# Attention maxima as two half-height matmuls side by side, four score banks, and the values one group later

## The chip, the cores and the metric

The kernel runs on one core of a Trainium2 chip. The metric is the device time of one launch in microseconds (us); lower is better. The core's engines are called PE (TensorE), DVE (VectorE), ACT (ScalarE), POOL (GpSimd) and SP (SyncE, which here only issues DMAs).

## The reference, cut to what matters

The program is two layers: a linear attention with a quantised feed-forward, then a softmax attention over 4096 tokens with 16 heads of 16, then a mixture of experts. The change touches only the softmax attention:

```
q, k, v = heads of layer_norm(x) @ Wq, Wk, Wv, with rotary positions on q and k     # 16 heads x 4096 x 16
p = softmax(q @ k.T * 16 ** -0.5)                                                   # 4096 x 4096 for each head
att = p @ v
```

## The kernel before

`attention` computes the softmax attention in bf16 products of split numbers. q and k are each the sum of three bf16 parts, and six products of parts (`Q_PART`, `K_PART`) stand under each other as rows of `QS` and `KS`: 6 x 16 = 96 rows (`ROWS`), so that one matmul over 96 rows sums all six. Two more rows hold the negative row maximum (in two bf16 parts) in `QS` and ones in `KS`, so that a score comes out of PE already shifted.

The work is 4 groups of 4 heads, and in each group 8 blocks of 512 queries: 32 blocks, numbered n. A block has 32 rounds (u), one for every 128 keys. In a round PE issues:
- four scores (`score`, L1068): 128 keys x 512 queries for one head each, into one of three PSUM banks `ST`. ACT takes the exponential of each (L1151) into the ring `PT` of 12.
- the values (`weigh`, L1083): four fp32 matmuls, one for each head, each on 32 of the array's columns, that sum into `OT`.
- two pairs of maxima matmuls (`max_pair`, L1049), for a *later* block: q times k over 96 rows, 128 queries x 512 keys twice, into a slot of two banks of `MP`. DVE takes one maximum over the 1024 numbers (L1179). There are two slots, so DVE can read one while PE fills the other.

The maxima of a block run 12 pairs (`LEAD`) and up to a block ahead. When all 64 pairs of the block are done, DVE makes the shift rows (`shifts`, L1184 to L1187), PE transposes them in round 29 (`negmax_transpose`), DVE copies them (`spread`), and SP puts them into `QS` (`store_negmax`). The output of the block before is copied out of `OT` by ACT (L1162), transposed by PE in round 2 (`out_transpose`, L1062), normalised by DVE (`normalise`, L1201 and L1203) and stored. Before the first block there is a head: SP loads group 0 and group 1 (`load_group`), and the 64 pairs of block 0 and 12 of block 1 run alone.

The order on each engine is the order of the code; semaphores carry the dependences. `mp_free` counts the maxima slots given back, `mp_full` those filled, `exp_done` the exponentials, `av_done` the rounds of values. ACT runs its 31 first blocks as a hardware loop (`act.Fori`, L1166), DVE its 30 first, PE six of the eight blocks of each group.

## Time and profile before

| | us |
|---|---|
| median of 3 runs (4894.16 to 4898.21) | 4896.37 |
| the profiled execution, its own time | 4870.05 |
| its span in the trace | 4868.0 |
| PE busy (93% of the span) | 4549.9 |
| DVE busy (63%) | 3049.8 |
| ACT busy (57%) | 2754.2 |
| POOL busy (8%) | 382.0 |

The profiled execution ran 26 us below the median, so durations read from it are summed against 4870.05. Busy PE time is an upper bound, since the ends of pipelined matmuls are modelled: what an instruction costs its successor is read from the starts. Shares are means over stages with different limits; the attention is the stretch from about 623 to 3782 us.

### The profile page before, as it was taken

The page shows a single profiled execution, that of the slowest core. Times are in us where ns is not written, and L with a number is a line of the kernel's source. Part 1 is how long each engine was busy: PE and PEld are TensorE (multiplying, and loading weights), DVE is VectorE, ACT ScalarE, POOL GpSimd, SP SyncE. Part 2 cuts the span into 40 slices and gives each one's busy share as a digit, 9 for nine tenths or more (in the row PEclk, how much of TensorE's full clock was granted, in tenths as well). Part 3 has the DMA queues.
Part 4 walks back from the last instruction along what each step waited for, and adds up shares of the span by engine and source line. Part 5 has one row for each costly group of instructions (what it writes and reads, how often), then busy time and mean ns, then how long its engine had stood idle before and what let it go on. Part 6 is the DMA issues. An engine that isn't in the chain of part 4 may idle for free. (4 is left out here: it accounts for less than half of the span.)

```text
span 4868.0 us, 75623 instructions
## 1 busy us (share of the span) xinstructions
PE 4549.9 (93%) x23944; PEld 2044.3 (42%) x23944; DVE 3049.8 (63%) x3267; ACT 2754.2 (57%) x5129; POOL 382.0 (8%) x364
## 2 busy tenths in 40 slices
PE   6888659999999999999999999999999799999999
PEld 4566402222222222222222222222222588886666
DVE  6777468888788878878887888888782011112222
ACT  4454306777777777777777777777778223222222
POOL 1233443000000000000000000000000100002110
PEclk8998759999999999999999999999999899999999
DMA  4222392000004000002200000000000655541111
GB/s 136 79 86 83 106 159 84 3 2 2 3 2 71 2 3 2 2 3 27 47 2 3 2 2 2 3 2 2 3 2 2 232 200 187 198 144 47 61 61 39
DMA packets 212703, 254.64 MB, mean 52 GB/s; under 512 B 35888, under 2 KB 183600, under 8 KB 210896
## 3 DMA queue, kind: packets, MB, share of 16 engines
q1 hardware_dynamic: 202544, 221.62, 16.3%
q0 software_dynamic: 9888, 30.04, 2.0%
q8 instruction: 93, 1.52, 0.1%
q14 instruction: 178, 1.46, 0.1%
HBM read 180.57 MB, written 70.78 MB: 52 GB/s over the span
## 5 line engine op out<-in xcount | busy, mean ns | idle before, releaser
L1179 DVE TENSOR_REDUCE a_MX<-a_MP 128x1 f32<-128x1024 f32 x2048 | 2415.8, 1220 | 584.3 <-PE a_MP L1049 577.3
L1151 ACT ACTIVATE a_PT<-a_ST 128x512 f32<-128x512 f32 x4096 | 2193.0, 598 | 970.6 <-PE a_ST L1068 904.6
L1068 PE MATMUL a_ST<-a_QS,a_KS 98*128 (+1 forms) x4096 | 1398.7, 385 | 70.3 <-ACT a_PT L1151 70.2
L1049 PE MATMUL a_MP<-a_KS,a_QS 96*128 96x512 bf16 x4096 | 1268.9, 392 | 58.1 <-DMA a_KS<-scr_kparts 44.5
L1083 PE MATMUL a_OT<-a_PT,a_VG 128*32 128x512 f32 x8192 | 1115.3, 617 | 0.1
L1068 PEld LDWEIGHTS a_ST<-a_QS,a_KS 98*128 98x128 bf16 x4096 | 394.9, 97 | 1272.0 <-ACT a_PT L1151 815.9
L1049 PEld LDWEIGHTS a_MP<-a_KS,a_QS 96*128 (+1 forms) x4096 | 385.9, 99 | 541.5 <-DVE a_MX L1179 130.7
L1384 ACT ACTIVATE e_hT<-e_up,e_BF 128x256 f32<-128x256 f32 x312 | 148.0, 474 | 409.8 <-PE e_up L1337 409.7
L1083 PEld LDWEIGHTS a_OT<-a_PT,a_VG 128*32 128x32 f32 x8192 | 162.0, 108 | 427.5 <-ACT a_PT L1151 388.3
L1337 PE MATMUL e_up<-e_xT,e_WF 128*128 128x256 f32 x1248 | 323.5, 382 | 0.8 <-DVE e_xT L1394 0.8
L1346 PE MATMUL e_dn<-e_WP,e_hT 128*128 128x256 f32 x1248 | 321.3, 380 | 0.0
L1346 PEld LDWEIGHTS e_dn<-e_WP,e_hT 128*128 128x128 f32 x1248 | 237.7, 191 | 33.1
L1337 PEld LDWEIGHTS e_up<-e_xT,e_WF 128*128 128x128 f32 x1248 | 236.2, 192 | 32.2 <-DVE e_xT L1394 1.2
L1280 POOL MEMSET e_ident<- 128x128 f32 x1 | 0.2, 204 | 2981.6 <-POOLq L908 2981.6
L1394 DVE COPY e_xT<-e_tp 128x512 f32<-128x512 f32 x39 | 27.0, 692 | 297.1 <-PE e_tp L1330 297.1
L1672 DVE TENSOR_TENSOR u_Y<-u_w,t_XN 128x512 f32<-128x512 f32 x16 | 11.1, 692 | 313.6 <-PE u_w L1577 313.6
L1401 DVE TENSOR_TENSOR e_Y<-e_dn,e_BP 128x256 f32<-128x256 f32 x78 | 32.1, 424 | 235.5 <-PE e_dn L1346 235.3
L342 ACT ACTIVATE f_E<-f_F 128x512 f32<-128x512 f32 x128 | 79.4, 620 | 137.9 <-PE f_F L581 137.9
L1646 ACT ACTIVATE u_hT<-u_a,t_bfs 128x512 f32<-128x512 f32 x64 | 44.0, 687 | 187.1 <-PE u_a L1589 187.1
L1646 ACT ACTIVATE u_hT<-u_a,t_b1c 128x512 f32<-128x512 f32 x64 | 44.0, 687 | 164.7 <-PE u_a L1589 164.7
L467 DVE SCALAR_TENSOR_TENSOR f_QP<-f_E,f_R 128x512 f32<-128x512 f32 x128 | 99.4, 801 | 46.9 <-ACT f_R L343 46.6
L1599 PE MATMUL u_d<-t_wps,u_hT 128*128 128x256 f32 x512 | 121.0, 379 | 0.0
(219 smaller groups left out, 2796.2 us busy)
## 6 DMA issues: line engine op xcount, KB each, us to landing
e_WF<-Wfc SPq DMA_DIRECT2D x39, 1024.0 KB, 5.0
e_WP<-Wproj SPq DMA_DIRECT2D x39, 1024.0 KB, 7.1
a_QS<-scr_qparts SPq DMA_DIRECT2D x192, 64.0 KB, 14.9
a_KS<-scr_kparts SPq DMA_DIRECT2D x24, 512.0 KB, 19.3
scr_xs<-f_zero SPq DMA_DIRECT2D x1, 9984.0 KB, 32.8
e_XS<-scr_xs SPq DMA_DIRECT2D x39, 256.0 KB, 2.7
scr_ys<-e_Y SPq DMA_DIRECT2D x39, 256.0 KB, 2.1
f_X<-x SPq DMA_DIRECT2D x16, 512.0 KB, 4.8
```

The costliest lines, as they stand in the source:

```text
L342: A.activation(E[:, u % ER, :], F[:, j, :], ACT.Exp)
L467: V.scalar_tensor_tensor(QP[:, g // 2 * 4 + j, g % 2, :], E[:, u % ER, :], 1.0, R[:, u % ER, :], ALU.min, ALU.add).then_inc(S["feat"], 1)
L1049: last = T.matmul(MP[:, slot, i, :], QS[j][0:ROWS, bass.ds((b * HG + h) * BLK + t * P, P)], KS[j][0:ROWS, h, (kb + i) * BLK:(kb + i + 1) * ...
L1068: T.matmul(ST[:, bank_of(c), :], KS[j][:, h, u * P:(u + 1) * P], QS[j][:, bass.ds((b * HG + h) * BLK, BLK)], start=True, stop=True).then_i ...
L1083: last = T.matmul(OT[w, :], VG[j][:, u, w], PT[:, (HG * u + h) % RING, :], start=u == 0, stop=u == KT - 1)
L1151: nc.scalar.activation(PT[:, c % RING, :], ST[:, bank_of(c), :], ACT.Exp, scale=SOFT_SCALE).then_inc(S["exp_done"], 1)
L1179: V.reduce_max(MX[:, x:x + 1], MP[:, slot, :, :].rearrange("p a n -> p (a n)"), AX.X).then_inc(S["mp_free"], 1)
L1337: last = T.matmul(UP[:, m % UPB, 0:ET], WF[j][:, k, m * P:(m + 1) * P], xT[j][:, k, :], start=k == 0, stop=k == DC - 1)
L1346: last = T.matmul(DN[:, t, 0:D], hT[j][:, m, t * P:(t + 1) * P], WP[j][:, m, :], start=m == 0, stop=m == HC - 1)
L1384: nc.scalar.activation(hT[j][:, m, :], UP[:, m % UPB, 0:ET], ACT.Gelu_apprx_tanh, bias=BF[j][:, m:m + 1]).then_inc(S["hid_ready"], 1)
L1599: last = T.matmul(DN[:, t // 2, t % 2 * D:(t % 2 + 1) * D], hT[:, u % HR, t * P:(t + 1) * P], down_w[half][:, m, :], start=u == 0 and t % ...
L1646: nc.scalar.activation(hT[:, u % HR, :], A[:, use % BANKS, :], ACT.Relu if u >= HC else ACT.Gelu_apprx_tanh, bias=(tt["b1c"] if u >= HC el ...
```

## The change

The rows of `QS` and `KS` are laid out anew, on all 128 rows. For the first two heads of a group (side 0) the first four products stand in rows 0 to 63, the last two in rows 64 to 95 and the shift rows from row 96; for the other two heads (side 1) the four products stand in rows 64 to 127, the two in rows 0 to 31 and the shifts from row 32. The rows left over are zero in `QS` (POOL writes them once).

A pair of maxima is now one head of each side for the same 512 keys: two matmuls over 64 rows each, one on the upper and one on the lower half of the array's rows, each into a bank of its own. The maximum is taken over four products, not six (it only shifts the exponent, so the softmax stays the same). `MP` is three single banks in a ring instead of two double ones; DVE takes one maximum over 512 numbers for each bank, and `mp_free` counts banks. The bank that this frees makes a fourth score bank.

A round on PE is now pair, values, pair, four scores; the values are those of the group of four scores before, and the last values of a block are issued in the first round of the next one. PE and DVE are written out without loops; ACT keeps its loop. Loads of `QS` and `KS` and the store of the shifts are split by side, so there are twice as many DMAs of half the size, and the head's first maxima wait for the four leading products only.

```
-STACK = ROWS + SHIFTS
+HALF = 64
+LEADING = HALF // HD1
+SIDES = HG // 2
 CHUNKS = HG * KT
-SBANKS = 3
-PAIRS = HG * TPB * KB // 2
+SBANKS, MBANKS = 4, 3
+PAIRS = HG // 2 * TPB * KB
 LEAD = 12
 TURN_OUT = 2
 TURN_MAX = 29
-EVENTS = PAIRS + 2
-HEAD_EVENTS = PAIRS + 1 + LEAD
+EVENTS = SIDES * PAIRS + 2
...
+HEAD_EVENTS = SIDES * (PAIRS + LEAD) + 1
...
-EXPS = 2 * SBANKS
...
-    return max(c for c in range(chunk - 2 * SBANKS, chunk) if bank_of(c % CHUNKS) == bank_of(chunk))
+def main_row(side, r):
+    return HD1 * r + HALF * side if r < LEADING else HD1 * (r - LEADING) + HALF * (1 - side)
+def shift_row(side):
+    return HALF * (1 - side) + HD1 * (len(Q_PART) - LEADING)
+def first_event(n):
+    return HEAD_EVENTS + n * EVENTS - (SIDES * LEAD if n == NG * NB - 1 else 0)
...
-        MP = pb("MP", [P, 2, 2, BLK])
+        MP = pb("MP", [P, MBANKS, BLK])
         OT = pb("OT", [P, BLK])
-        def negT_ps(slot):
-            return MP[:, slot, 0, :].bitcast(bf16)[0:SHIFTS * HG * TPB, 0:P]
+        def bank(e):
+            return MP[:, e % MBANKS, :]
...
-                nc.gpsimd.memset(KS[j][ROWS:STACK, :, :], 1.0).then_inc(S["ones_ok"], 1)
-                pool.wait_ge(S["ones_ok"], j + 1)
...
+                for side in range(SIDES):
+                    r0, h0 = shift_row(side), side * HS
+                    nc.gpsimd.memset(KS[j][r0:r0 + WIN, h0:h0 + HS, :], 1.0).then_inc(S["ones_ok"], 1)
+                    nc.gpsimd.memset(QS[j][r0:r0 + WIN, :].rearrange("r (b h n) -> r b h n", b=NB, h=HG)[:, :, h0:h0 + HS, :],
+                                     0.0).then_inc(S["ones_ok"], 1)
+            pool.wait_ge(S["ones_ok"], 4 * SIDES)
...
+                for side in range(SIDES):
+                    h0, row = G * HG + side * HS, main_row(side, r)
+                    heads, c0 = slice(h0 * HD1, (h0 + HS) * HD1), (b * HG + side * HS) * BLK
+                    sp.dma_start(QS[G % 2][row:row + HD1, c0:c0 + HS * BLK].rearrange(
+                        "e (h n) -> e h n", h=HS), scr["qparts"][Q_PART[r], heads, b * BLK:(b + 1) * BLK].rearrange(
+                        "(h e) n -> e h n", e=HD1)).then_inc(sem, 16)
...
-                early = S["first"] if G == 0 else load[G % 2]
                 for r in range(len(Q_PART)):
+                    early = S["first"] if G == 0 and r < LEADING else load[G % 2]
                     load_q(G, r, 0, early)
...
-                sp.dma_start(QS[j][ROWS:STACK, bass.ds(b * HG * BLK, HG * BLK)], negT[:]).then_inc(S["negmax_load"], 16)
+                for side in range(SIDES):
+                    rows = SHIFTS * HS * TPB
+                    sp.dma_start(QS[j][shift_row(side):shift_row(side) + SHIFTS, bass.ds((b * HG + side * HS) * BLK, HS * BLK)],
+                                 negT[side * rows:(side + 1) * rows, :]).then_inc(S["negmax_load"], 16)
...
+            sp.wait_ge(S["ones_ok"], 4 * SIDES)
             store_negmax(0, 0, 0)
...
-                room(e)
-                for i in range(2):
-                    last = T.matmul(MP[:, slot, i, :], QS[j][0:ROWS, bass.ds((b * HG + h) * BLK + t * P, P)],
-                                    KS[j][0:ROWS, h, (kb + i) * BLK:(kb + i + 1) * BLK], start=True, stop=True)
-                last.then_inc(S["mp_full"], 1)
...
+                h, t, kb = x // (TPB * KB), x // KB % TPB, x % KB
+                room(e + SIDES - 1)
+                for side in range(SIDES):
+                    hs, half = side * HS + h, slice(side * HALF, (side + 1) * HALF)
+                    T.matmul(bank(e + side), QS[j][half, bass.ds((b * HG + hs) * BLK + t * P, P)],
+                             KS[j][half, hs, kb * BLK:(kb + 1) * BLK], start=True, stop=True).then_inc(S["mp_full"], 1)
...
-            def score(n, j, b, c):
-                u, h = c // HG, c % HG
-                pe.wait_ge(S["exp_done"], n * CHUNKS + freed_by(c) + 1 + EXPS)
-                T.matmul(ST[:, bank_of(c), :], KS[j][:, h, u * P:(u + 1) * P],
-                         QS[j][:, bass.ds((b * HG + h) * BLK, BLK)], start=True, stop=True).then_inc(S["qk_done"], 1)
-            def score_first(n, j, b):
-                pe.wait_ge(S["negmax_load"], 16 * (n + 1))
-                for c in range(SBANKS):
-                    score(n, j, b, c)
-            def weigh(n, j, u):
-                pe.wait_ge(S["exp_done"], n * CHUNKS + HG * u + HG - 1 + EXPS + 1)
...
+            def scores(n, j, b, u):
+                for c in range(HG * u, HG * (u + 1)):
+                    pe.wait_ge(S["exp_done"], n * CHUNKS + c + 1)
+                    h = c % HG
+                    T.matmul(ST[:, c % SBANKS, :], KS[j][:, h, u * P:(u + 1) * P],
+                             QS[j][:, bass.ds((b * HG + h) * BLK, BLK)], start=True, stop=True).then_inc(S["qk_done"], 1)
+            def scores_first(n, j, b):
+                pe.wait_ge(S["negmax_load"], 16 * SIDES * (n + 1))
+                scores(n, j, b, 0)
+            def weigh(n, u):
+                j = n // NB % 2
+                pe.wait_ge(S["exp_done"], n * CHUNKS + HG * (u + 1) + SBANKS)
...
                 for u in range(KT):
-                    for x in range(2 * u, 2 * u + 2):
+                    for x in (2 * u, 2 * u + 1):
                         if x < PAIRS - LEAD and next1:
-                            max_pair(first + k, (HEAD_EVENTS + k) % 2, *next1, x + LEAD)
-                            k += 1
+                            max_pair(e, *next1, x + LEAD)
+                            e += SIDES
                         if x >= PAIRS - LEAD and next2:
-                            max_pair(first + k, (HEAD_EVENTS + k) % 2, *next2, x - PAIRS + LEAD)
-                            k += 1
+                            max_pair(e, *next2, x - PAIRS + LEAD)
+                            e += SIDES
                         if x % 2 == 0:
-                            score(n, j, b, HG * u + SBANKS)
                             if u:
-                                weigh(n, j, u - 1)
+                                weigh(n, u - 1)
+                            elif n:
+                                weigh(n - 1, KT - 1)
                             if u == TURN_OUT:
-                                out_transpose(first + k, (HEAD_EVENTS + k) % 2, n)
-                                k += 1
+                                out_transpose(e, n)
+                                e += 1
                             if u == TURN_MAX and next1:
-                                negmax_transpose(first + k, (HEAD_EVENTS + k) % 2, n + 1)
-                                k += 1
-                            if u < KT - 1:
-                                score(n, j, b, HG * u + SBANKS + 1)
+                                negmax_transpose(e, n + 1)
+                                e += 1
                     if u < KT - 1:
-                        score(n, j, b, HG * u + SBANKS + 2)
-                        score(n, j, b, HG * u + SBANKS + 3)
-                if next1:
-                    score_first(n + 1, *next1)
-                weigh(n, j, KT - 1)
-            pe.wait_ge(S["ident_ok"], 1)
-            pe.wait_ge(S["ones_ok"], 2)
+                        scores(n, j, b, u + 1)
+                    elif next1:
+                        scores_first(n + 1, *next1)
...
-                with pe.Fori(0, NB - 2) as b:
+                for b in range(NB - 2):
...
+            weigh(NG * NB - 1, KT - 1)
+            out_transpose(first_event(NG * NB - 1) + 1, NG * NB)
...
+            def maximum(e, x):
+                for side in range(SIDES):
+                    dve.wait_ge(S["mp_full"], e + side + 1)
+                    V.reduce_max(MX[:, side, x:x + 1], bank(e + side), AX.X).then_inc(S["mp_free"], 1)
...
-            with dve.Fori(0, NG * NB - 2) as n:
-                one_block(n, True, True)
...
+            blocks = NG * NB
+            for n in range(blocks):
+                one_block(n, n + 1 < blocks, n + 2 < blocks)
```

On PE, one round in the middle of a block. Before (`a_ST` are the scores, `a_MP` the maxima, `a_OT` the values):

```order
L1068 MATMUL a_ST<-a_QS,a_KS 128x512
L1049 MATMUL a_MP<-a_KS,a_QS 128x512 x2
L1068 MATMUL a_ST<-a_QS,a_KS 128x512 x2
L1049 MATMUL a_MP<-a_KS,a_QS 128x512 x2
L1068 MATMUL a_ST<-a_QS,a_KS 128x512
L1083 MATMUL a_OT<-a_PT,a_VG 32x512 x4
```

And one round on PE now:

```order
L1073 MATMUL a_MP<-a_KS,a_QS 128x512 x2
L1106 MATMUL a_OT<-a_PT,a_VG 32x512 x4
L1073 MATMUL a_MP<-a_KS,a_QS 128x512 x2
L1092 MATMUL a_ST<-a_QS,a_KS 128x512 x4
```

The scores moved together at the round's end, and the values stand between the two pairs.

On PE, where a block ends and the next begins, with the semaphores that each waits for. Before:

```order
L1068 MATMUL a_ST<-a_QS,a_KS 128x512 [waits a_exp_done,a_negmax_load]
L1068 MATMUL a_ST<-a_QS,a_KS 128x512 [waits a_exp_done] x2
L1083 MATMUL a_OT<-a_PT,a_VG 32x512 [waits a_exp_done]
L1083 MATMUL a_OT<-a_PT,a_VG 32x512 x3
L1049 MATMUL a_MP<-a_KS,a_QS 128x512 [waits a_mp_free]
L1049 MATMUL a_MP<-a_KS,a_QS 128x512
L1068 MATMUL a_ST<-a_QS,a_KS 128x512 [waits a_exp_done] x2
L1049 MATMUL a_MP<-a_KS,a_QS 128x512 [waits a_mp_free]
L1049 MATMUL a_MP<-a_KS,a_QS 128x512
```

And the same place on PE now:

```order
L1092 MATMUL a_ST<-a_QS,a_KS 128x512 [waits a_exp_done,a_negmax_load]
L1092 MATMUL a_ST<-a_QS,a_KS 128x512 [waits a_exp_done] x3
L1073 MATMUL a_MP<-a_KS,a_QS 128x512 [waits a_mp_free]
L1073 MATMUL a_MP<-a_KS,a_QS 128x512
L1106 MATMUL a_OT<-a_PT,a_VG 32x512 [waits a_exp_done]
L1106 MATMUL a_OT<-a_PT,a_VG 32x512 x3
L1073 MATMUL a_MP<-a_KS,a_QS 128x512 [waits a_mp_free]
L1073 MATMUL a_MP<-a_KS,a_QS 128x512
L1092 MATMUL a_ST<-a_QS,a_KS 128x512 [waits a_exp_done] x4
```

Between the block's last values and the first scores that need an exponential from beyond ACT's jump there was one pair and three scores; the last values now come behind the first pair of the next block.

## Rows read from the trace of the kernel before

**Rows 1.** The page's groups: line, engine, operation, count, busy us, mean ns, idle before

```profile
L1179 DVE TENSOR_REDUCE a_MX<-a_MP 128x1 f32<-128x1024 f32 x2048 | 2415.8, 1220 | 584.3 <-PE a_MP L1049 577.3
...
L1394 DVE COPY e_xT<-e_tp 128x512 f32<-128x512 f32 x39 | 27.0, 692 | 297.1 <-PE e_tp L1330 297.1
...
L1401 DVE TENSOR_TENSOR e_Y<-e_dn,e_BP 128x256 f32<-128x256 f32 x78 | 32.1, 424 | 235.5 <-PE e_dn L1346 235.3
```

**Rows 2.** Timeline of one round: start us, us, engine, what, count, idle before

```profile
3650.30 0.39 PE L1068 MATMUL a_ST<-a_QS,a_KS 98*128 98x512 bf16 x1
...
3650.53 0.60 PE L1049 MATMUL a_MP<-a_KS,a_QS 96*128 96x512 bf16 x2
...
3650.81 2.15 ACT L1151 ACTIVATE a_PT<-a_ST 128x512 f32<-128x512 f32 x4 [0.69 <-PE a_ST L1068]
...
3651.16 2.36 DVE L1179 TENSOR_REDUCE a_MX<-a_MP 128x1 f32<-128x1024 f32 x2 [0.48 <-PE a_MP L1049]
...
3651.83 0.38 PE L1068 MATMUL a_ST<-a_QS,a_KS 98*128 98x512 bf16 x1
...
3652.14 1.06 PE L1083 MATMUL a_OT<-a_PT,a_VG 128*32 128x512 f32 x8
...
3653.14 0.39 PE L1068 MATMUL a_ST<-a_QS,a_KS 98*128 98x512 bf16 x1
```

**Rows 3.** Timeline where one block ends and the next begins, and one block later

```profile
1222.91 0.60 ACT L1162 COPY a_OS<-a_OT 128x512 f32<-128x512 f32 x1
...
1225.64 1.57 ACT L1151 ACTIVATE a_PT<-a_ST 128x512 f32<-128x512 f32 x3 [2.13 <-issue]
...
1226.39 0.39 PE L1068 MATMUL a_ST<-a_QS,a_KS 98*128 x1 [2.00 <-ACT a_PT L1151]
...
1318.41 0.60 ACT L1162 COPY a_OS<-a_OT 128x512 f32<-128x512 f32 x1
```

**Rows 4.** Busy time by stretch; PEclk is the granted clock as a share

```profile
core 0: us, PE busy (x) PEld busy (x) DVE busy (x) ACT busy (x) POOL busy (x), PEclk, DMA share, GB/s
1224.30:1226.40 2.10, 0.10 (x2) 0.01 (x1) 1.40 (x2) 0.76 (x2) 0.00 (x0) 1.00 0.01 4
1226.40:1229.70 3.30, 3.30 (x12) 0.63 (x12) 1.22 (x1) 1.91 (x4) 0.00 (x0) 0.56 0.00 0
3710.00:3770.00 60.00, 53.56 (x303) 11.60 (x301) 0.68 (x2) 51.63 (x100) 0.00 (x0) 1.00 0.01 3
623.00:640.00 17.00, 0.00 (x0) 0.00 (x0) 0.00 (x0) 0.00 (x0) 16.94 (x2) 0.50 0.98 115
```

**Rows 5.** Groups with shapes, 1000 to 1500 us: DVE's work once in a block

```profile
L1203 DVE TENSOR_TENSOR a_AO<-a_MP,a_rd 128x256 f32<-128x256 f32 x5 | 2.1, 425 | 0.7
L1184 DVE TENSOR_REDUCE a_neg<-a_MX 128x16 f32<-128x64 f32 x6 | 1.3, 220 | 0.2
L1201 DVE RECIPROCAL a_rd<-a_MP 128x16 f32<-128x16 f32 x5 | 1.3, 258 | 1.6 <-PE a_MP L1062 1.6
```

**Rows 6.** Timeline of PE in round 2 of block 0: the output's transposes

```profile
757.13 0.66 PE L1062 MATMUL a_MP<-a_identf,a_OS 128*128 128x128 f32 x4
757.62 0.38 PE L1068 MATMUL a_ST<-a_QS,a_KS 98*128 x1
```

**Rows 7.** Timeline of the head: first load issued, first maxima, last load issued

```profile
623.09 0.35 SPq L981 DMA_DIRECT2D a_QS<-scr_qparts  x1
...
656.81 1.86 PE L1049 MATMUL a_MP<-a_KS,a_QS 96*128 96x512 bf16 x4 [44.53 <-DMA a_KS<-scr_kparts]
...
657.86 75.31 DVE L1179 TENSOR_REDUCE a_MX<-a_MP 128x1 f32<-128x1024 f32 x64 [35.41 <-PE a_MP L1049]
...
725.89 0.46 SPq L992 DMA_DIRECT2D a_VG<-scr_va  x1
```

**Rows 8.** Timeline of ACT: the last block's start, one of its rounds, its end

```profile
3704.01 0.60 ACT L1162 COPY a_OS<-a_OT 128x512 f32<-128x512 f32 x1
...
3712.68 2.06 ACT L1151 ACTIVATE a_PT<-a_ST 128x512 f32<-128x512 f32 x4 [0.33 <-PE a_ST L1068]
...
3780.64 0.59 ACT L1162 COPY a_OS<-a_OT 128x512 f32<-128x512 f32 x1 [1.19 <-PE a_OT L1083]
```

More of the change, by code:

```diff
@@ L1189, in spread @@
-            def spread(n, e, slot, after):
-                dve.wait_ge(S["mp_full"], e + 1)
-                if after:
-                    dve.wait_ge(S["negmax_load"], n * 16)
-                V.tensor_copy(negT[:], negT_ps(slot)).then_inc(S["negmaxT_copied"], 1)
+            dve.sem_inc(S["mp_free"], MBANKS)
+            def maximum(e, x):
+                for side in range(SIDES):
+                    dve.wait_ge(S["mp_full"], e + side + 1)
+                    V.reduce_max(MX[:, side, x:x + 1], bank(e + side), AX.X).then_inc(S["mp_free"], 1)
@@ L1194, in spread, with normalise @@
+            def spread(n, e):
+                dve.wait_ge(S["mp_full"], e + 1)
+                if n:
+                    dve.wait_ge(S["negmax_load"], n * 16 * SIDES)
+                V.tensor_copy(negT[:], negT_ps(e)).then_inc(S["negmaxT_copied"], 1)
                 dve.wait_ge(S["negmaxT_copied"], n + 1)
                 dve.sem_inc(S["mp_free"], 1)
-            def normalise(n, e, slot):
+            def normalise(n, e):
                 dve.wait_ge(S["mp_full"], e + 1)
-                o4 = MP[:, slot, 0, :].rearrange("p (t h e) -> p t h e", t=TPB, h=HG)
+                o4 = bank(e).rearrange("p (t h e) -> p t h e", t=TPB, h=HG)
@@ L1208, in one_block @@
             def one_block(n, more1, more2):
-                c.base, c.n, k = FIRST + n * STEPS, 0, 0
-                first = HEAD_EVENTS + n * EVENTS - (0 if more1 else LEAD)
+                e = first_event(n)
                 for u in range(KT):
-                    for x in range(2 * u, 2 * u + 2):
+                    for x in (2 * u, 2 * u + 1):
                         if x < PAIRS - LEAD and more1:
-                            maximum(first + k, (HEAD_EVENTS + k) % 2, x + LEAD)
-                            k += 1
+                            maximum(e, x + LEAD)
+                            e += SIDES
@@ L1216, in one_block @@
                             if x == PAIRS - LEAD - 1:
-                                shifts(n + 1, first + k - 1)
+                                shifts(e)
                         if x >= PAIRS - LEAD and more2:
-                            maximum(first + k, (HEAD_EVENTS + k) % 2, x - PAIRS + LEAD)
-                            k += 1
+                            maximum(e, x - PAIRS + LEAD)
+                            e += SIDES
                         if x == 2 * TURN_OUT:
-                            normalise(n, first + k, (HEAD_EVENTS + k) % 2)
@@ L1223, in one_block @@
-                            k += 1
+                            normalise(n, e)
+                            e += 1
                         if x == 2 * TURN_MAX and more1:
-                            spread(n + 1, first + k, (HEAD_EVENTS + k) % 2, True)
-                            k += 1
+                            spread(n + 1, e)
+                            e += 1
             for x in range(PAIRS):
-                maximum(x, x % 2, x)
-            shifts(0, PAIRS - 1)
-            spread(0, PAIRS, PAIRS % 2, False)
+                maximum(SIDES * x, x)
@@ L1232, in _ @@
+            shifts(SIDES * PAIRS)
+            spread(0, SIDES * PAIRS)
             for x in range(LEAD):
[L1233 to L1241 removed]
```

99 lines of the change are left out of this document (43 added, 56 removed).

## The prediction

> **What bounds the kernel now.** I read the page's groups first. DVE's maxima are its costliest work, 2048 of 1220 ns, yet DVE was idle 577 us of its time waiting for PE's maxima [rows 1]. So DVE is not the bound; it is second in line. The timeline of one round says the same with starts: PE goes from score to score in 3653.14 - 3650.30 = 2.84 us without a hole, DVE works 2.36 of that and waits 0.48, ACT 2.15 and waits 0.69 [rows 2]. PE is the bound of a round. Its parts: two matmuls of 512 columns end 0.60 after the first starts and one alone takes 0.385, so one costs its successor 0.215; eight of them (four scores, four maxima) are 1.72. From the last score to the values it is 0.31 (3652.14 - 3651.83), 0.10 above 0.215. The values take 1.00 to the next start. 1.72 + 0.10 + 1.00 = 2.82.
>
> Then the timeline at a block's end. From copy to copy a block takes 1318.41 - 1222.91 = 95.50 us [rows 3], against 32 rounds of 2.84 = 90.9. Of the 4.6 left, 0.49 are the output's transposes (757.62 - 757.13) [rows 6]. Most of the rest starts at ACT: after its copy it jumps back in its loop and takes its next exponential 2.73 us later (1225.64 - 1222.91), and PE stands 2.00 us for it [rows 3]. Right behind that hole PE's granted clock is 0.56 for 3.3 us, where it had been 1.00: half of the time it is at 1.2 instead of 2.4 GHz [rows 4]. That costs about 3.3 x 0.44 = 1.5 us of PE's work.
>
> **What the change does to PE's round.** A pair of maxima stands on two halves of the rows. If the halves run at once, a pair costs one matmul, 0.215, and not two. No row shows two row halves. The nearest are the values, which use four column strips of 32: four fp32 matmuls in 1.00 us [rows 2], and the trace counts eight passes of 512 columns in them; one after another at 0.215 they would be 1.72, so strips do run at once. I take 0.245 (0.03 for loading the second half's weights, an estimate). Bounds: 0.215, and 0.43 if the halves don't overlap.
>
> Against that, PE changes its tiling more often. Before, it did so twice in a round: into the values (+0.10) and out of them (1.00 less 4 x 0.215 is 0.14, an estimate, if the values stream as long as four scores). Now it is four times: maxima to values, values to maxima, maxima to scores, scores to maxima. I price the two new ones at 0.12 each, the mean of the two known. The sum: 0.245 + 0.10 + 1.00 + 0.245 + 0.12 + 0.86 + 0.12 = 2.69, say 2.70. With changes at 0.10 and a pair at 0.215 it is 2.59; with new changes at 0.20 and a pair at 0.245 it is 2.85.
>
> The Trainium skill, "TensorEngine Tiling (Array Packing)", Key Properties, says that changing the tiling mode drains TensorE, which speaks against this order of the round; the extra 0.10 and 0.14 beside the values agree. By its Theoretical Speedup a contraction of up to 64 gives up to 2x, so it expects the halves to overlap.
>
> **DVE's round.** It now takes four maxima over 512 numbers for two over 1024. A read of 512 instead of 256 numbers costs 692 - 424 = 268 ns more, so 512 numbers are 536 ns [rows 1]. One maximum alone is then 1220 - 536 = 684 ns. In the head 64 of the long ones ran back to back in 75.31 us, 1.177 each [rows 7]; short ones back to back are 0.641, four are 2.56. DVE's floor is below PE's 2.70, but only by 0.14, where it was 0.48.
>
> Does the ring of three banks let both run? Let pair A start at 0. DVE can start 0.42 after the last matmul of a pair (3651.16 - 3650.53 - 0.215) [rows 2], so at about 0.45. PE reaches pair B at 0.245 + 0.10 + 1.00 = 1.35; B needs A's first bank, which is read at 0.45 + 0.68 = 1.13. B is there at 1.80, DVE is through with A at 1.73. The next A comes at 2.70 and needs B's first bank, read at 2.48. So both handovers fit with about 0.2 us to spare, and PE sets the round. But only 0.2: before, a whole slot was between them.
>
> So DVE's work once in a block is no longer covered. Normalising is 258 + 425 ns and two waits on itself, some 0.85 [rows 5], beside 0.49 of transposes on PE [rows 6]; DVE reads the next pair only after that, I count 1.0 for both. The shifts are 220 ns and three small ones behind it, 0.85, of which 0.2 is covered: 0.65. Spread and its transpose: 0.3. Together 2.0 a block.
>
> **The block's end.** ACT still loops, so the 2.73 us from copy to next exponential stay. But the last values now stand behind the first pair of the next block, and four scores are out already. With that pair at 0, the values start at 0.35, the copy at about 1.6, ACT's next exponential at 4.3, done at 4.9. PE meanwhile has a pair, four scores whose banks are free, a pair, the values of group 0 and a pair; it comes to the first score that needs that exponential at 4.4, and then takes one score for each exponential, 0.52 apart (2.15 less 0.60, by three), instead of 0.215. The stall is 0.5 + 3 x 0.3 = 1.4 us instead of 2.0, and in pieces. I add 0.6 for a clock that falls behind some of them: 2.0.
>
> A block is 32 x 2.70 + 2.0 + 2.0 = 90.4, which is 5.1 less than 95.5. There are 31 such, 158 us.
>
> **Last block.** No maxima there: 3780.64 - 3704.01 = 76.6 us, of which each round is 2.06 of exponentials and 0.33 of waiting for a score [rows 8]. With four banks and the values a group behind, PE's 1.96 (0.10 + 1.00 + 0.86) lies beside ACT's 2.07, so about 32 x 2.07 + 1 = 67: 9 us. The six rounds without maxima before it give 1 more.
>
> **Head.** Loads are bound by the DMA engines, 0.98 busy from 623 to 640 us [rows 4], so half-size DMAs of the same bytes cost the same. The first maxima wait for four of six products: two thirds of the 33.7 us from 623.09 to 656.81, 11 us sooner [rows 7]. At the head's 1.2 GHz [rows 4] the ring of three is too short: DVE needs 1.28 for a pair, and a pair of matmuls at this clock is ready 657.86 - 656.81 - 0.43 = 0.62 after its last one starts. With 0.03 for the halves and 0.05 for the semaphore (estimates) that is 0.70 from the end of a first read, a little over the 0.64 of the second read that covers it. So about 1.33 against 1.177, times 76 pairs: 12 us more. Net nothing. SP issues 218 DMAs instead of 109 ahead of the first shifts. It took 103 us for the 109 (725.89 - 623.09), held up by full DMA engines; one issue by itself is 0.35 long [rows 7], so 218 are at least 76 us and may still fit. I take nothing, with up to +20. POOL's extra clearing lies beside the head.
>
> **Sum.** -158 - 9 - 1 + 0 = -168 against 4870.05, so 4702. The median stood 26 us above the profiled execution: 4728, say 4725.
>
> **Rivals.**
> - *The halves don't overlap.* A pair costs 0.43, the round 2.69 + 2 x 0.185 = 3.06, a block 102; 31 x 6.5 - 10 = +190: about 5085. For it: no row shows row halves. Against: the column strips do overlap. It decides from a pair above 0.33. Chance 0.06.
> - *The handover is the bound.* If the new changes of tiling cost 0.20, or a bank comes back 0.2 us later than I count, each pair waits: 2.85 a round, a block 95.2, about 4875. For it: only 0.2 to spare, DVE 95% full. Against: PE's waits in the head are short. Chance 0.12, half of it within 0.2% of no change or slower.
> - *The block's end stays as it is.* The clock falls at every end and PE waits as before, 2 us a block more: 4725 + 60 = 4785. Chance 0.14.
> - *SP's queue.* If issuing costs by the DMA and not by the byte, the first shifts wait for up to 100 us more behind group 1's loads: about 4790. Chance 0.04.
> - *The clock falls in the rounds.* PE is then full 2.13 of 2.70; but in the last block it ran at clock 1.00 with 1.72 of 2.39 [rows 4, 8]. Half clock would be slower, over 5500. Chance 0.01.
> - *As forecast*: 0.63.
>
> **How the numbers follow.** A measurement of this kernel tells about 0.2% from no change, 10 us. Faster: 0.63 + 0.14 + 0.04 + half of 0.12 = 0.87. Slower: 0.06 + 0.01 + 0.02 = 0.09. Same: 0.04. The forecast's own range comes from the round: 2.59 gives 4725 - 31 x 32 x 0.11 = 4616, and 2.76 gives 4785. The handover rival ends at 4875. Cutting the low end at 4640 and the high end at 4840 leaves about 2 in 10 out.
>
> **What would show it.** In the changed trace: the two matmuls of a pair start within 0.05 us of each other and the pair costs its successor under 0.3; a round is 2.70 from values to values; DVE's short maximum is 684 ns and DVE is over 90% busy in the attention; ACT's copy-to-exponential gap still 2.7 us but PE's idle behind it under 1 us in one piece; a block 90.4, the last one 67. I am wrong if a change of tiling costs much more than 0.12, or if PE is seen waiting for DVE before most pairs.

## The result, and the profile after

The changed kernel takes 4626.88 us (median of 4 runs, 4626.26 to 4627.09) against 4895.26 us (4 runs, 4885.17 to 4898.21) for the kernel before on the same chip: a ratio of 0.9451, 95% interval 0.9437 to 0.9466. The prediction was 4725 with a range from 4640 to 4840. The sign was right, the time is 98 us under the forecast and 13 us under the range. The profiled execution took 4626.26 us, so the gain between profiled executions is 243.8 us where 168 were worked out.

The page's groups of the changed kernel, in the columns of [rows 1]:

```profile
L1199 DVE TENSOR_REDUCE a_MX<-a_MP 128x1 f32<-128x512 f32 x4096 | 2631.5, 685 | 144.9 <-PE a_MP L1073 84.2
L1171 ACT ACTIVATE a_PT<-a_ST 128x512 f32<-128x512 f32 x4096 | 2108.4, 605 | 810.4 <-PE a_ST L1092 519.3
```

DVE's idle time in front of its maxima fell from 584 us [rows 1] to 145: the spare time is gone, and a short maximum is 685 ns where 684 was worked out.

The timeline of one round of the changed kernel, as [rows 2] for before:

```profile
1501.28 0.39 PE L1073 MATMUL a_MP<-a_KS,a_QS 64*128 64x512 bf16 x2
...
1501.60 1.07 PE L1106 MATMUL a_OT<-a_PT,a_VG 128*32 128x512 f32 x8
...
1502.60 0.39 PE L1073 MATMUL a_MP<-a_KS,a_QS 64*128 64x512 bf16 x2
...
1502.92 1.04 PE L1092 MATMUL a_ST<-a_QS,a_KS 128*128 128x512 bf16 x4
1503.43 1.57 ACT L1171 ACTIVATE a_PT<-a_ST 128x512 f32<-128x512 f32 x3 [0.55 <-PE a_ST L1092]
1503.89 0.39 PE L1073 MATMUL a_MP<-a_KS,a_QS 64*128 64x512 bf16 x2
```

The x2 of a pair spans 0.39, as one matmul alone did in [rows 2], where two in a row spanned 0.60: the halves run at once, with no lag to be seen. From the starts a round is 0.32 + 1.00 + 0.32 + 0.97 = 2.61 us, and nothing in it waits. The four scores are 4 x 0.215 = 0.86 of the 0.97, the pair 0.215 of each 0.32. So each change of tiling next to a pair costs 0.10 to 0.11.

The end of a block in the changed kernel, to be held against [rows 3]; the last row is the copy one block later:

```profile
1212.99 0.59 ACT L1182 COPY a_OS<-a_OT 128x512 f32<-128x512 f32 x1
...
1215.39 0.39 PE L1073 MATMUL a_MP<-a_KS,a_QS 64*128 64x512 bf16 x2
1215.65 4.03 ACT L1171 ACTIVATE a_PT<-a_ST 128x512 f32<-128x512 f32 x8 [2.08 <-PE a_OT L1106]
...
1216.30 1.86 PE L1092 MATMUL a_ST<-a_QS,a_KS 128*128 128x512 bf16 x4 [0.53 <-ACT a_PT L1171]
...
1218.09 0.39 PE L1073 MATMUL a_MP<-a_KS,a_QS 64*128 64x512 bf16 x2
...
1300.09 0.59 ACT L1182 COPY a_OS<-a_OT 128x512 f32<-128x512 f32 x1
```

From ACT's copy to its next exponential it is 2.66 us, nearly as before (2.73). PE stands 0.53 in one piece and then takes a score for each exponential: from pair to pair it is 2.70 (1218.09 - 1215.39) where a group of scores otherwise takes 1.29 (1503.89 - 1502.60), so 1.41 are lost. A block is 1300.09 - 1212.99 = 87.10 us, 8.4 less than [rows 3].

Busy time by stretch, in the columns of [rows 4]: 500 us of full blocks, then the stretches at and behind PE's wait.

```profile
1000.00:1500.00 500.00, 480.13 (x2913) 124.14 (x2968) 480.16 (x776) 381.19 (x741) 0.00 (x0) 1.00 0.05 7
...
1215.60:1218.90 3.30, 2.47 (x16) 0.64 (x14) 1.85 (x4) 3.25 (x7) 0.00 (x0) 1.00 0.01 2
1218.90:1222.00 3.10, 2.69 (x19) 0.92 (x12) 2.62 (x6) 1.93 (x5) 0.00 (x0) 1.00 0.01 2
```

DVE is 0.96 busy, and the granted clock stays 1.00 behind the block's end, where it was 0.56 before [rows 4]. The busy share overstates how full DVE is: a maximum is 0.69 long in the trace, but where DVE has maxima to catch up on (behind the normalising, at 1220.96) they start 0.60 to 0.61 apart. Four of them take about 2.43 of the round's 2.61, so DVE has some 0.18 to spare in each round.

The copies of the last blocks and ACT inside the last one, as [rows 8]:

```profile
3390.52 0.59 ACT L1182 COPY a_OS<-a_OT 128x512 f32<-128x512 f32 x1
3472.58 0.62 ACT L1182 COPY a_OS<-a_OT 128x512 f32<-128x512 f32 x1
...
3499.57 12.88 ACT L1171 ACTIVATE a_PT<-a_ST 128x512 f32<-128x512 f32 x26
...
3535.74 0.58 ACT L1182 COPY a_OS<-a_OT 128x512 f32<-128x512 f32 x1 [1.19 <-PE a_OT L1106]
```

The last block is 63.16 us against 76.6. ACT no longer waits in it: exponentials in a row cost 12.88 / 26 = 0.495 each, 1.98 a round. The block ahead of it is 82.06.

The head of the changed kernel, as [rows 7]:

```profile
621.79 0.81 SPq L998 DMA_DIRECT2D a_QS<-scr_qparts  x2
...
642.34 0.61 PE L1073 MATMUL a_MP<-a_KS,a_QS 64*128 64x512 bf16 x2 [31.34 <-DMA a_KS<-scr_kparts]
643.73 0.61 PE L1073 MATMUL a_MP<-a_KS,a_QS 64*128 64x512 bf16 x2 [0.78 <-DVE a_MX L1199]
...
733.30 0.21 DVE L1214 COPY a_negT<-a_MP 32x128 bf16<-32x128 bf16 x1 [0.56 <-issue]
737.78 0.43 SPq L1011 DMA_DIRECT2D a_VG<-scr_va  x1
738.33 6.26 SPq L1030 DMA_DIRECT2D a_QS<-a_negT  x2
...
750.69 1.49 PE L1092 MATMUL a_ST<-a_QS,a_KS 128*128 128x512 bf16 x3 [1.60 <-DMA a_QS<-a_negT]
```

First maxima 20.6 us behind the first load, against 33.7 in [rows 7]; pairs at 1.39; the shifts ready at 733.5 and on their way only at 738.33, behind SP's last load. PE stands 1.60 us for them.

Between first scores and first copy, block 0 showed something that the trace of before did not have:

```profile
785.41 0.96 POOL L983 DMA_INDIRECT scr_xs<-a_XR,g_slot  x1 [0.30 <-issue]
786.26 1.29 DVE L1199 TENSOR_REDUCE a_MX<-a_MP 128x1 f32<-128x512 f32 x2 [2.42 <-remote]
786.40 2.06 ACT L1171 ACTIVATE a_PT<-a_ST 128x512 f32<-128x512 f32 x4 [2.67 <-remote]
...
787.01 0.39 PE L1073 MATMUL a_MP<-a_KS,a_QS 64*128 64x512 bf16 x2 [2.20 <-issue]
```

DVE, ACT and PE stand still together, released by nothing that the trace names ("remote", "issue"), again and again while POOL scatters token rows for the experts (it does so from 688 to 817 us). All three are idle at once in six places of more than 0.5 us before the first copy, 0.7 to 2.8 us each; the rest of the loss is waits of one engine at a time. The first copy stands at 864.57 in place of 842.77.

### The profile page after: what moved, and what is told of

It reads as the page before. It is cut to its first block and busy times, and to the rows that moved or that the text cites. A ratio compares the mean times of both kernels' runs of the same rounds, so it can differ in the third digit from the quotient of the medians.

```text
span 4624.5 us, 70156 instructions
## 1 busy us (share of the span) xinstructions
PE 4221.0 (91%) x23643; PEld 1849.4 (40%) x23944; DVE 3267.1 (71%) x5315; ACT 2670.8 (58%) x5129; POOL 409.1 (9%) x370
## 5 line engine op out<-in xcount | busy, mean ns | idle before, releaser
L1199 DVE TENSOR_REDUCE a_MX<-a_MP 128x1 f32<-128x512 f32 x4096 | 2631.5, 685 | 144.9 <-PE a_MP L1073 84.2
L1171 ACT ACTIVATE a_PT<-a_ST 128x512 f32<-128x512 f32 x4096 | 2108.4, 605 | 810.4 <-PE a_ST L1092 519.3
L1106 PE MATMUL a_OT<-a_PT,a_VG 128*32 128x512 f32 x8192 | 1093.9, 606 | 1.2 <-ACT a_PT L1171 0.9
L1092 PE MATMUL a_ST<-a_QS,a_KS 128*128 128x512 bf16 x3795 | 1033.4, 383 | 56.9 <-ACT a_PT L1171 23.6
L1073 PE MATMUL a_MP<-a_KS,a_QS 64*128 64x512 bf16 x4096 | 817.0, 396 | 153.8 <-DVE a_MX L1199 105.7
L1073 PEld LDWEIGHTS a_MP<-a_KS,a_QS 64*128 64x128 bf16 x4096 | 196.9, 93 | 1403.3 <-DVE a_MX L1199 1341.0
L1092 PEld LDWEIGHTS a_ST<-a_QS,a_KS 128*128 128x128 bf16 x4096 | 319.9, 98 | 551.4 <-ACT a_PT L1171 279.3
```

What stands on the lines that cost most here:

```text
L1073: T.matmul(bank(e + side), QS[j][half, bass.ds((b * HG + hs) * BLK + t * P, P)], KS[j][half, hs, kb * BLK:(kb + 1) * BLK], start=True, sto ...
L1092: T.matmul(ST[:, c % SBANKS, :], KS[j][:, h, u * P:(u + 1) * P], QS[j][:, bass.ds((b * HG + h) * BLK, BLK)], start=True, stop=True).then_i ...
L1106: last = T.matmul(OT[w, :], VG[j][:, u, w], PT[:, (HG * u + h) % RING, :], start=u == 0, stop=u == KT - 1)
L1171: nc.scalar.activation(PT[:, c % RING, :], ST[:, c % SBANKS, :], ACT.Exp, scale=SOFT_SCALE).then_inc(S["exp_done"], 1)
L1199: V.reduce_max(MX[:, side, x:x + 1], bank(e + side), AX.X).then_inc(S["mp_free"], 1)
```

## The experiments

Ratios are against the kernel before on the same chip. The runs were made on three chips. On one the kernel before takes 4867 us: there ran the experiments with both matmuls on one half, with half maxima, with ACT written out (first run) and with the late scatter. On the two others it takes 4891. The changed kernel itself was not run on the first chip, so what is held against it there goes by the ratio and by the length of a block, not by the time. The base for all is the changed kernel, run again on one of the two others:

> The changed kernel itself once more (one blank line added), as the base for the runs beside it. If the changed kernel's time is a fixed share of the kernel before's on any chip: ratio 0.945. In block 0 the first profile had holes of 1 to 3.5 us in which DVE, ACT and PE stood still together, some 22 us in all. Theory 1, the holes belong to that one execution or chip: none here, the first copy of OT 842 to 850 us into the span. Theory 2, they belong to the kernel (the scatter runs beside block 0): the first copy near 864 us and a hole of over 1 us wherever the scatter runs.

Measured: 4626.22 us, ratio 0.9459 [0.9446, 0.9472]; first copy at 859.88, blocks 87.10, last block 63.15. The holes showed again.

### Do the two halves run at once?

```
-                for side in range(SIDES):
+                side = x % 2
+                for i in range(2):
+                    y = x // 2 * 2 + i
+                    h, t, kb = y // (TPB * KB), y // KB % TPB, y % KB
                     hs, half = side * HS + h, slice(side * HALF, (side + 1) * HALF)
-                    T.matmul(bank(e + side), QS[j][half, bass.ds((b * HG + hs) * BLK + t * P, P)],
+                    T.matmul(bank(e + i), QS[j][half, bass.ds((b * HG + hs) * BLK + t * P, P)],
```

> The two maxima matmuls of a pair stand on the same half of the rows (two key blocks of one head) and not on both halves; the work and the order are otherwise the changed kernel's. If the gain of a round comes from the two halves running at once, the second matmul costs 0.215 again: a round 2.61 + 2 x 0.215 = 3.04 us, the kernel 4627 + 992 x 0.43 = about 5055 us. Rival, the gain comes from the order and the banks alone: 4627, no change.

Measured: 4976.59 us, ratio 1.0233 [1.0216, 1.0250]. PE's timeline:

```profile
1500.65 0.60 PE L1075 MATMUL a_MP<-a_KS,a_QS 64*128 64x512 bf16 x2
1501.18 1.06 PE L1108 MATMUL a_OT<-a_PT,a_VG 128*32 128x512 f32 x8
1502.18 0.60 PE L1075 MATMUL a_MP<-a_KS,a_QS 64*128 64x512 bf16 x2
1502.71 1.04 PE L1094 MATMUL a_ST<-a_QS,a_KS 128*128 128x512 bf16 x4
1503.68 0.60 PE L1075 MATMUL a_MP<-a_KS,a_QS 64*128 64x512 bf16 x2
```

On one half the pair spans 0.60 and costs 0.215 more (0.53 to the values in place of 0.32), the round is 3.03, as expected. A block is 99.43, 12.3 more and not 13.8: beyond its 32 rounds a block now has 2.4 us where it had 3.6, which fits that a slower PE covers part of DVE's work once in a block again. So the halves do overlap, wholly, and without that the change would have made the kernel slower. The rival that they don't is refuted.

### Does PE or DVE set the round?

```
-                    V.reduce_max(MX[:, side, x:x + 1], bank(e + side), AX.X)
+                    V.reduce_max(MX[:, side, x:x + 1], bank(e + side)[:, 0:BLK // 2], AX.X)
```

> DVE takes its maxima over 256 of the 512 numbers (so the shift is not the row's true maximum); the output changes only by rounding. If PE sets the round, it stays 2.61 us and only DVE's once-a-block work gets covered: a block 87.1 to about 85.5, the head's 76 pairs shorter by 0.27 each, in all some 4555. Rival, DVE (96% busy) sets the round: it falls by more than 0.05, and the kernel below 4520.

Measured: 4563.79 us, ratio 0.9382 [0.9363, 0.9401]; DVE 0.58 busy from 1000 to 1500 us, the starts in a round unchanged (0.32, 1.00, 0.32, 0.97), a block 85.70. It leaves out half of each maximum. PE sets the round; of the block, 1.4 us are DVE's. The ratio is 0.008 above what the expectation comes to (4555 of 4895), and half of that is the head: the shifts were ready at 719.1, but SP's store of them stood behind its loads. SP's and PE's timeline, up to 752 us:

```profile
739.59 6.11 SPq L1030 DMA_DIRECT2D a_QS<-a_negT  x2
...
751.43 1.06 PE L1092 MATMUL a_ST<-a_QS,a_KS 128*128 128x512 bf16 x2 [19.66 <-DMA a_QS<-a_negT]
```

From first load to first scores it was 127.8 us, where the changed kernel takes 128.9: faster maxima do not shorten the head, since SP's queue is right behind them.

### What does a change of tiling cost?

```
                         if x % 2 == 0:
+                            if u < KT - 1:
+                                scores(n, j, b, u + 1, 0, 2)
                             if u:
                                 weigh(n, u - 1)
...
-                        scores(n, j, b, u + 1)
+                        scores(n, j, b, u + 1, 2, HG)
```

> The first two of the four scores stand ahead of the values, so that a round has five changes of tiling (pair to scores, scores to values, values to pair, pair to scores, scores to pair) and not four, with the same matmuls. Theory: each change costs PE 0.10 us: the round 2.61 to 2.71, a block 87.1 to 90.3, in all some 100 us slower than the control. By the 0.12 of the prediction it would be 120 us slower. Rival: a change costs nothing by itself, and what stands ahead of the values (0.32 from pair to values) is theirs: round 2.61, no difference.

Measured: 5058.55 us, ratio 1.0341 [1.0325, 1.0356]: four times the loss that was expected. PE's timeline shows where:

```profile
1500.56 0.39 PE L1073 MATMUL a_MP<-a_KS,a_QS 64*128 64x512 bf16 x2
1500.88 0.61 PE L1092 MATMUL a_ST<-a_QS,a_KS 128*128 128x512 bf16 x2
1501.74 0.39 PE L1073 MATMUL a_MP<-a_KS,a_QS 64*128 64x512 bf16 x2 [0.24 <-DVE a_MX L1201]
1502.06 0.60 PE L1092 MATMUL a_ST<-a_QS,a_KS 128*128 128x512 bf16 x2
1502.59 1.07 PE L1106 MATMUL a_OT<-a_PT,a_VG 128*32 128x512 f32 x8
1503.59 0.39 PE L1073 MATMUL a_MP<-a_KS,a_QS 64*128 64x512 bf16 x2
```

The steps without a wait are 0.32 or 0.53 (2 x 0.215 + 0.10) or 1.00: a fifth change is 0.10 again. But the two pairs now stand 1.18 and 1.85 apart, and the first distance is a wait for a bank. The round is 3.03, 0.10 from the change and 0.32 from the handover. A block is 100.5, 13.4 more, and 1.1 to 1.6 longer still where the granted clock falls at its end, which it does behind 22 of the 30 ends: of the 432 us that were lost, some 30 are the clock. What the 0.10 of a change is made of, no run takes apart. To part the change from the wait, the same order with a shorter read:

```
 five changes as above, and
+                    V.reduce_max(MX[:, side, x:x + 1], bank(e + side)[:, 0:BLK // 2], AX.X)
```

> The round with five changes of tiling again (two of the four scores ahead of the values), now with DVE's maxima over 256 of the 512 numbers (it leaves half of each maximum out), so that a bank comes back sooner. In the run with whole maxima the starts read 0.32 from pair to scores, 0.53 for two scores, 1.00 for the values: 0.10 for each change, in sum 2.71 a round, and 0.32 more of waiting for a bank, since a pair can follow a pair only 1.18 behind it (0.43 until DVE starts, 0.68 its read, 0.07 back to PE). Theory: with the read at 0.42 that falls to 0.92, nothing waits, and the round is 2.71 against 2.61 of the half maxima alone: a block 85.7 + 3.2 = 88.9, ratio 0.938 + 0.021 = 0.959. Rival: the wait is not for a bank but part of the changes themselves: round 3.03 as with whole maxima, ratio about 1.03.

Measured: 4789.86 us, ratio 0.9798 [0.9783, 0.9813]. The round went from 3.03 to 2.76: the wait was for the bank, since only DVE's read was shortened. Of the 0.05 over 2.71, all stands between the two pairs that are close (0.90 apart, under the 0.92 that I had worked out), so a trace of the wait is left. The total missed 0.959: a block is 92.2, not 88.9. Its rounds are 88.3; 2.2 is what the block with half maxima alone has beyond its rounds (85.7 - 83.5, of which 1.4 is the block's end); and 1.7 is new. Most of it stands at the block's end: with two scores ahead of the values PE comes sooner to a score that needs an exponential from beyond ACT's jump, and stands 2.2 to 2.5 us in one piece (2.42 at 1053.39) where it stood 0.5. Besides, 7 of the 29 full blocks are 1.3 to 1.6 longer still; in just these the granted clock falls at the end (below).

### What the fourth score bank is worth

```
-SBANKS, MBANKS = 4, 3
+SBANKS, MBANKS, EARLY = 3, 3, 4
...
-                    pe.wait_ge(S["exp_done"], n * CHUNKS + c + 1)
+                    pe.wait_ge(S["exp_done"], n * CHUNKS + freed_by(c) + 1 + EXPS)
...
-                    T.matmul(ST[:, c % SBANKS, :], KS[j][:, h, u * P:(u + 1) * P],
+                    T.matmul(ST[:, bank_of(c), :], KS[j][:, h, u * P:(u + 1) * P],
```

(`bank_of` is the chunk modulo 3, `freed_by` the chunk that read the bank last.)

> Three score banks in place of four (the maxima keep their three single banks, one bank of PSUM lies idle), all else as changed. Theory: the fourth bank is what lets the four scores stand together. With three, the fourth score of a group waits for the exponential of the first, which is ready about 0.51 + 0.61 us behind its score (score to exponential, one exponential), where the fourth score would start 0.65 behind it: some 0.45 us more in every round, 2.61 to about 3.05, and a block 87.1 to about 101; in all 31 x 14 = 430 us slower than the control. Rival: the scores stand in a queue with slack and PE makes up for the wait in the values: round 2.61, under 40 us slower.

Measured: 5153.52 us, ratio 1.0533 [1.0515, 1.0552], 527 us over the control. The fourth score waits for the first exponential:

```profile
1539.66 0.82 PE L1102 MATMUL a_ST<-a_QS,a_KS 128*128 128x512 bf16 x3
1540.82 0.39 PE L1102 MATMUL a_ST<-a_QS,a_KS 128*128 128x512 bf16 x1 [0.34 <-ACT a_PT L1181]
1541.14 0.39 PE L1083 MATMUL a_MP<-a_KS,a_QS 64*128 64x512 bf16 x2
```

It starts 1.16 behind the first in place of 0.65: 0.51 more, a round of 3.12. The direction and the mechanism were as expected, the size 0.07 a round short. (At 12 of the 30 block ends the clock falls too, for 1.3 us each.) The last block is 76.12 there, as before the change (76.6 [rows 8]), against 63.15 in the control: that saving belongs to the fourth bank.

### The block's end and the clock

```
-            with act.Fori(0, NG * NB - 1) as n:
+            for n in range(NG * NB - 1):
```

> ACT's blocks are written out, without its loop. If the stall at a block's end is ACT's jump, 1.4 us of each of 30 ends go: 4627 - 42 = 4585, and a block 85.7. Rival, ACT would start no sooner because it waits for the values or the copy: 4627.

Measured: 4556.96 us, ratio 0.9362 [0.9347, 0.9378]; on another chip (second run, below) 0.9375 [0.9362, 0.9387]. A block is 85.68, 1.42 less: the whole of PE's loss at the block's end is ACT's jump. (In us it is less than the 4585 that were expected since it ran on the chip where the kernel before takes 4867.)

Whether such a wait also costs clock, I tried by making it longer: ACT takes two exponentials of the next block ahead of its jump, not four.

```
-                for c in range(SBANKS, CHUNKS):
+                for c in range(2, CHUNKS):
...
-                    for c in range(SBANKS):
+                    for c in range(2):
```

> ACT takes only two of the next block's exponentials ahead of its copy and jump, not four. The same work, but PE then has less to do while ACT jumps, so it stands in one long hole at each block's end instead of pieces: about 1.2 us more standing. Theory, from the kernel before (2.00 us of standing still, then the clock at 0.56 for 3.3 us): one hole of 2 to 3 us brings the granted clock down behind it, and a block is 87.1 + 1.2 + 1.5 = 89.8, in all some 80 us slower than the control. Rival, the clock stays 1.00 whatever PE does here: 87.1 + 1.2 = 88.3, some 37 us slower.

Measured: 4695.36 us, ratio 0.9601 [0.9586, 0.9616], 69 us over the control, between the two expectations, and the blocks say why. Two block ends, PE's hole in each, and the clock behind it:

```profile
1045.55 0.88 PE L1092 MATMUL a_ST<-a_QS,a_KS 128*128 128x512 bf16 x2 [2.80 <-ACT a_PT L1171]
...
1226.22 0.88 PE L1092 MATMUL a_ST<-a_QS,a_KS 128*128 128x512 bf16 x2 [2.72 <-ACT a_PT L1171]
```

```profile
1047.00:1050.00 3.00, 3.00 (x14) 0.54 (x6) 2.35 (x4) 1.76 (x4) 0.00 (x0) 0.56 0.00 0
...
1227.00:1229.00 2.00, 2.00 (x15) 0.56 (x15) 1.52 (x3) 1.61 (x4) 0.00 (x0) 1.00 0.00 0
```

Nearly the same hole, and once the clock falls to 1.2 GHz for most of the next 3 us, once it stays at 2.4. Of the 29 full blocks 16 are 88.7 to 89.0 and 13 are 90.1 to 90.5: 1.5 us for a fallen clock, behind 13 of 29 holes. 29 x 1.7 + 13 x 1.5 = 69. So a hole of this length does not always cost clock, and pieces of 0.5 to 0.8, as in the changed kernel, never did: its clock is 1.00 behind every block end, and its full blocks are 87.1 to 87.3 in both runs.

Nor does the length decide it. Counted over the 30 block ends of each trace, the clock fell behind 29 in the kernel before (holes of 1.8 to 2.2 us), behind 22 with five changes (1.9 to 2.2), behind 7 with five changes and half maxima (2.2 to 2.5), behind 12 with three banks (2.4 to 2.7) and behind 13 here (2.6 to 2.9). What decides whether one of these holes costs clock was not found.

### The holes of block 0

```
             pool.wait_ge(S["ones_ok"], 4 * SIDES)
+            pool.wait_ge(S["av_done"], 4 * KT)
             for b in range(NB):
```

> POOL's scatter of rows to the experts waits until three blocks are done; before, it ran beside the head and block 0, where PE, DVE and ACT stand still together for 1 to 3.5 us at a time, 27 us in all. If the scatter's DMAs hold up the instruction fetch of the written-out code, the holes move with it, and the time stays at 4627 +- 5. If the holes belong to the start of the attention and need more than the scatter, they are gone from block 0 and don't come back: about 4602.

Measured: 4604.53 us, ratio 0.9466 [0.9450, 0.9482]: no gain. The chip was one without holes: its neighbours, with the scatter beside block 0, had none either (first copies 841 to 850), and the moved scatter made none (blocks 87.1 to 87.5). It was tried again, with ACT written out, beside ACT written out alone:

> ACT written out, and POOL's scatter of token rows starts behind block 3 instead of beside the head and block 0. Theory 1, the holes in block 0 come from the scatter's DMAs beside it, on a chip where they show: 22 us less than ACT written out alone on the same chip, no hole in block 0, first copy of OT near 836. Theory 2, the scatter has nothing to do with them: the same time as ACT written out alone, holes where they were.

> ACT written out once more (one blank line added), as the base on the same chip for the two runs before it: ratio 0.936, blocks 85.68. If the holes in block 0 show on this chip, the first copy of OT stands near 862, else near 842.

Measured: 4596.31 us, ratio 0.9400 [0.9387, 0.9413], with the late scatter, and 4583.17 us, ratio 0.9375 [0.9362, 0.9387], without. Here the holes show: without the late scatter the first copy stands 241.5 us behind the first load (864.31 - 622.79), with it 219.3 (840.36 - 621.02), the 22 us that were expected. But the copies around the scatter's new place are 1011.73 and 1137.67, 125.9 apart instead of 85.7:

```profile
1015.00:1137.00 122.00, 96.55 (x495) 21.89 (x496) 80.48 (x130) 63.99 (x123) 67.46 (x71) 0.85 0.32 103
```

The same stretch in the kernel beside it, with no scatter in it:

```profile
1015.00:1137.00 122.00, 119.32 (x736) 30.79 (x738) 118.80 (x195) 94.19 (x183) 0.00 (x0) 1.00 0.02 3
```

Theory 1 is right on the place, wrong on the gain: the holes follow the scatter, and cost 40 us when all of it lies beside full blocks, 22 when part of it lies beside the head. On the chip where the kernel before takes 4867 the same scatter costs at most 0.4 us a block. Why chips differ in this was not settled, nor whether code written out or in loops makes a difference: the one trace of the kernel before has the scatter beside block 0 and no holes, but it may come from a chip without them.

### The rest of DVE's work

```
+            for n in range(BY_POOL, NG * NB):
+                pool.wait_ge(S["neg_ready"], n - BY_POOL + 1)
+                c.step(nc.gpsimd.tensor_copy(negparts[:, :, 0, :], sides))
+                c.step(nc.gpsimd.tensor_tensor(sides, sides, negparts[:, :, 0, :], ALU.subtract))
+                nc.gpsimd.tensor_copy(negparts[:, :, 1, :], sides).then_inc(S["negmax_ready"], 1)
```

> ACT written out, and in blocks 4 and later POOL makes the shift rows from DVE's reduced maxima (copy, subtract, copy on 128 rows of 16 numbers) in place of DVE. Theory: DVE's three small operations are work that nothing covers, about 0.5 of the 0.85 us of the shifts: a block 85.68 to 85.1 to 85.2, in all 15 us less than ACT written out alone, ratio 0.933. Rival: POOL's way there and back is longer than DVE's, the transpose of the shifts in round 29 waits on PE and everything behind it with it: a block over 85.7, no gain or a loss of some 10 us.

Measured: 4566.31 us, ratio 0.9339 [0.9326, 0.9351], 17 us under ACT written out on the same chip. Where POOL makes the shifts, a block is 85.18 to 85.19, with one exception (85.33). POOL's way is no longer than DVE's as far as PE can tell. This is the best version found: 0.9339 against 0.9459 of the control, some 59 us less.

## Why the prediction was right in direction and wrong in size

- **PE's round, the step that failed.** I predicted 2.70 with "0.245 + 0.10 + 1.00 + 0.245 + 0.12 + 0.86 + 0.12"; it is 2.61. The mechanism was right, the prices too high: each pair costs 0.215, not 0.245 (the 0.03 for the second half's weights rested on no row, and no lag showed), the two new changes of tiling 0.10 to 0.11 each, not 0.12, and the sum was rounded up. 0.09 x 32 x 31 = 89 us, the largest part of the miss, and enough to put the time outside the range. The bound with both at their lowest was 2.59, so the rows held the answer; the range, cut at 4640, did not reach it.
- **The handover.** Right that PE, not DVE, sets the round, and that the margin is thin: two pairs must stand at least 1.18 apart, the changed kernel has them 1.29 and 1.32 apart. The two runs with five changes show what happens below that. DVE's own floor was put too high: 0.641 a maximum in a row, 2.56 a round, where 0.60 to 0.61 and 2.43 are seen. The length of one, 684 ns for a measured 685, was worked out from a copy and an addition, two different operations; that it fits to 1 ns is luck.
- **DVE's work once in a block.** Forecast 2.0. A block is 32 x 2.61 = 83.5 and 3.6 more, of which 1.4 is the block's end: 2.2, DVE's and the transposes' together. Nearly right.
- **The block's end.** The stall of 1.4 was right (1.41 from the timeline, 1.42 from writing ACT out). The 0.6 added for the clock was wrong: it never fell. That is 18 us over 30 blocks, set off in part by the 0.2 of the point above. The prediction also read a granted clock of 0.56 as 1.2 GHz for half of the time; between levels of 0.5 and 1.0 it is 0.88 of the 3.3 us. The 1.5 us that it took from the 0.56 does not hang on that, and a fallen clock cost 1.5 in the run with the long holes too. In the kernel before, the one full block without a fallen clock takes 93.85 between its copies, the others 95.4 to 95.8: so of the 8.4 us that a block gained, 7.2 are the rounds (32 x 0.226, by the median starts) and 1.6 the clock, which no longer falls; the shorter stall gives 0.6, and DVE's work, now uncovered, takes 1 back.
- **The tiling rule.** The Trainium skill, "TensorEngine Tiling (Array Packing)", Key Properties, has TensorE drain at a change of mode; the trace agrees in that each change costs 0.10, without showing what the 0.10 is. Its Theoretical Speedup, "Up to 2×" for a contraction of up to 64, is reached in full here: a pair costs what one matmul costs.
- **Last blocks.** Forecast 67, measured 63.2: exponentials in a row cost 0.495, and I had taken 2.07 / 4 = 0.517 from a row whose last one does not overlap a next. The block ahead of it gave 2.0 beyond a full block's 8.4, where I had 1.
- **Head.** To the first scores it is 750.69 - 621.79 = 128.9 against 125.0 before (748.07 - 623.09 in its timeline), where I predicted no difference. The earlier start gave 13 (forecast 11); a pair costs 1.39 (forecast 1.33), 16 us over 76 pairs (forecast 12; its 0.05 for the semaphore rested on no row); the shifts went out 4.8 late behind SP's loads, but 12 pairs run on PE meanwhile, and it stood only 1.6 for them (forecast 0 to 20). Right within 4 us. The count of 76 us for 218 issues was too low: in a row they start 0.47 apart (22 in 10.25 us, from 622.66), not 0.35.
- **Block 0.** From first scores to first copy 113.9, against 94.7: 19 us more where I forecast 5 less. That is the holes, which nothing in the trace of before announced: on the chip without holes it is 90.2 with the scatter in its new place (835.47 - 745.22, late scatter) and in its old one (842.13 - 751.88, ACT written out), 4.5 less than before, as forecast.
- **The sum.** From the first copy to the last the gain is 266.7 (2937.9 to 2671.2) where the forecast's terms give 163; up to the first copy 21.8 are lost where 5 were to be won; what follows differs by 1. Together 244 against 168. The other 22 us of the miss are the 26 that I added for the distance from profiled execution to median: there was none this time. It fits that the profiled execution of before came from a chip like the first one of the experiments (its 4870 against 4867 there, and no holes in its trace), and the median from one like the others; this was argued, not shown. If it is so, the 26 that were added and the 24 of the holes are the same thing on the two sides of this list and cancel, and the whole miss lies between the first copy and the last: 104 us, of which the round is 86, the clock 18 and the last blocks 6, less 6 for DVE's work.

## What to carry to other kernels

Two matmuls on separate 64-row halves cost here what one costs, so cutting a contraction to 64 rows can pay, with 0.10 us on the bill for each change of tiling between groups; count the changes of a loop and read each from start to start. Before reordering, work out the least distance at which a ring of banks can be filled again (here 1.18 us), and keep every distance above it: an order that looks 0.10 dearer cost 0.42. When several small prices are chosen between bounds and multiplied by a thousand rounds, the range has to reach to both bounds, not to a round number inside them.

## What the runs showed of the hardware that I had not expected

- The second half's matmul shows no lag at all behind the first: the pair spans 0.39, as one alone does.
- The clock behind a hole of 2.6 to 2.9 us fell in 13 of 30 cases, at 1.5 us each, behind one of 1.8 to 2.2 us in 29 of 30 (the kernel before) and in 22 of 30 (five changes); behind waits of 0.5 to 0.8 us in none.
- On two of three chips PE, ACT and DVE stand still together, for 0.7 to 3.6 us at a time, while POOL's indirect DMAs run; the scatter of this kernel costs 40 us in all beside full blocks. On the third chip they do not. The kernel before is 24 us slower on the first two as well.
- POOL's three small operations on 128 x 16 numbers are 0.20 to 0.22 us each beside a DVE that is 0.98 busy (1100 to 1500 us of that run), and moving them there took 0.5 us out of each block.
